# Two-layer steps of a conditional layer pair: the second gelu half ahead of x_hi on ScalarE, the second norm's statistics ahead of x_lo on VectorE

## What is computed

```python
out_nr  = gelu(x @ w1_nr + b1_nr) @ w2_nr + b2_nr          # out_tsr alike
out_sr  = gelu(gelu(x @ w1_sr + b1_sr) @ w2_sr + b2_sr) @ w3_sr + b3_sr
y = x + out[kind];  y = layernorm(y) * gamma + beta
h = gelu(y @ down_W.T + down_b)                            # 256 -> 64
h = h @ expert_W[e].T + expert_b[e] + domain_emb[e]
z = h @ up_W.T + up_b + y;  z = layernorm(z) * ln_gamma + ln_beta
```

## Time and profile before

| | |
|---|---|
| median of 3 runs | 278.79 us (278.51 to 279.04) |
| profiled execution | 277.94 us, its span 276.1 us |
| granted TensorE clock | 0.985 over the span, 1.00 in the two-layer steps from 120 to 240 us |
| PE busy | 252.9 us, 92% of the span |
| DVE busy | 203.0 us, 74% |
| ACT busy | 191.2 us, 69% |
| POOL busy | 174.7 us, 63% |
| chain that ended last | PE 58%, ACT 13%, issue 11%, DVE 8%, POOL 5% |

### The profile page before, as it was taken

The page is one execution under the profiler, slowest core; times in us unless marked ns, Lnnn a source line. Parts: engine busy times, 40 slices in busy tenths (PEclk is TensorE's granted clock), DMA queues, the critical chain, the costliest instruction groups (busy, mean ns, idle before and its releaser), DMA issues.

```text
span 276.1 us, 8026 instructions
## 1 busy us (share of the span) xinstructions
PE 252.9 (92%) x2114; PEld 219.2 (79%) x2115; DVE 203.0 (74%) x715; ACT 191.2 (69%) x450; POOL 174.7 (63%) x190
## 2 busy tenths in 40 slices
PE   7998999999999988999999999999999999999850
PEld 7798889989989977878887777788888888778630
DVE  6779453294495485878888877888888888878871
ACT  3587579668768765867777777777777777777730
POOL 3134565455876876867777677677776777677480
PEclk9999999999999999999999999999999999999995
DMA  6373011101212202232323222333232323222224
GB/s 181 101 251 70 6 36 42 23 22 40 61 39 58 67 28 57 67 85 80 91 76 95 76 76 79 83 85 82 80 85 77 94 76 95 76 77 71 54 66 92
DMA packets 41640, 20.71 MB, mean 75 GB/s; under 512 B 37431, under 2 KB 39181, under 8 KB 41614
## 3 DMA queue, kind: packets, MB, share of 16 engines
q1 hardware_dynamic: 37785, 12.23, 18.5%
q0 software_dynamic: 2592, 7.08, 7.3%
q10 hardware_dynamic: 1236, 1.06, 1.5%
HBM read 11.69 MB, written 8.65 MB: 74 GB/s over the span
## 4 chain that ended last, share of the span: by engine, by line
PE 58%; ACT 13%; issue 11%; DVE 8%; POOL 5%; DMA 2%; DVEq 1%; ACTq 1%; SPq 1%; POOLq 0%
PE ps_h L1082 18%; PE ps_z L1150 12%; PE ps_t L1172 9%; PE ps_z L1155 6%; ACT yt L931 5%; ACT x_hi L883 4%; ACT h_hi L897 3%; POOL h_lo L481 2%; PE ps_z L1117 2%; PE ps_u L1202 2%; PE ps_t L1253 2%; POOL rs L488 1%; PE ps_t L1256 1%; PE ps_t L1254 1%; DMA out<-o 1%
## 5 line engine op out<-in xcount | busy, mean ns | idle before, releaser
L481 POOL TENSOR_TENSOR h_lo<-h,h_hi 128x256 fp32r<-128x256 f32 (+1 forms) x75 | 70.6, 942 | 45.3 <-ACT h L897 42.1
L488 POOL TENSOR_TENSOR rs<-ve,minus_half 128x4 f32<-128x4 f32 (+1 forms) x38 | 41.0, 1079 | 32.2 <-DVE ve L699 32.0
L904 ACT ACTIVATE zn<-ps_z,nm,rs 128x256 f32<-128x256 f32 x66 | 33.7, 562 | 31.4 <-DVE nm L703 30.9
L687 DVE BATCH_NORM_STATS2 st<-ps_z 128x6 f32<-128x256 f32 x66 | 24.9, 418 | 31.5 <-PE ps_z L1155 31.5
L897 ACT ACTIVATE h_hi<-ps_h,per_feature_sb 128x256 fp32r<-128x256 f32 x84 | 38.9, 496 | 12.3 <-PE ps_h L1082 8.2
L931 ACT ACTIVATE yt<-ps_t,per_feature_sb 128x256 f32<-128x256 f32 x66 | 34.1, 574 | 17.5 <-PE ps_t L1172 17.4
L1150 PE MATMUL ps_z<-last_hi,h_hi 128*128 (+1 forms) x132 | 35.8, 305 | 6.7 <-ACT h_hi L897 6.7
L897 ACT ACTIVATE h<-ps_h,per_feature_sb 128x256 f32<-128x256 f32 x84 | 38.8, 498 | 0.0
L661 DVE TENSOR_TENSOR x_lo<-x,x_hi 128x512 fp32r<-128x512 f32 x33 | 23.5, 712 | 19.8 <-ACT x_hi L883 19.8
L1202 PE MATMUL ps_u<-tables,stack 65*64 x132 | 35.6, 392 | 0.3 <-ACT stack L915 0.3
L1202 PE MATMUL ps_u<-second_table,stack 65*64 65x256 f32 x132 | 35.5, 392 | 0.0
(11 more groups left out here) (150 smaller groups left out, 658.3 us busy)
## 6 DMA issues: line engine op xcount, KB each, us to landing
x<-in_x_feat SPq DMA_DIRECT2D x130, 64.0 KB
out<-o SPq DMA_DIRECT2D x20, 64.0 KB, 2.0
out<-o,out_rows_now POOLq DMA_INDIRECT x54
last_sb<-in_last_w SPq DMA_DIRECT2D x1, 768.0 KB, 5.0
w_sr_sb<-in_w_sr SPq DMA_DIRECT2D x1, 512.0 KB, 4.0
w_sr_sb<-in_w_sr ACTq DMA_DIRECT2D x1, 512.0 KB, 5.0
w_two_sb<-in_w_two SPq DMA_DIRECT2D x1, 512.0 KB, 5.6
per_unit_sb<-in_per_unit SPq DMA_DIRECT2D x1, 268.1 KB
```

The costliest lines, as they stand in the source:

```text
L481: pool.tensor_tensor(dst, full, high.bitcast(F32), ALU.subtract).then_inc(ready, 1)
L488: pool.tensor_tensor(RS[p][:, norms, :], VE[p][:, norms, :], half_of_two[:, norms, :], ALU.pow).then_inc(rstd, 1)
L904: ins = act.activation(ZN[:, t, :], ZP[p][:, t, :], ACT.Identity, bias=NM[p][:, t:t + 1], scale=RS[p][:, 0, t:t + 1])
```

## The change

On ScalarE, the two-layer branch makes the second gelu half before it makes x_hi of the slot after next. On VectorE, in all steps of the main loop and in LAST2, the second norm's statistics come before x_lo, and their aggregation stays behind it; in LAST2 the call to `last_variances` is written out accordingly. No instruction is added or taken away. The SR branch on ScalarE, and the programs of GpSimd, TensorE and SyncE, are as before.

```diff
                 for slot in on_slot(g, 0, where):
                     first_moments(slot, p)
                 variances(p, BOTH)
+                for slot in on_slot(g, 2, where):
+                    second_stats(slot, p)
                 for slot in on_slot(g, -2, where):
                     input_low(slot, p)
                 for slot in on_slot(g, 2, where):
+                    second_moments(slot, p, q)
                     if where == LAST2:
-                        last_variances(slot, p, q)
-                    else:
-                        second_stats(slot, p)
-                        second_moments(slot, p, q)
+                        dve.wait_ge(stat[1], 2 * TT * slot + 2 * TT)
+                        variances(q, SECOND)
@@
-                    next_input(g, i, p, where)
                     for k in kind:
                         second_of_two(k)
+                    next_input(g, i, p, where)
```

## The result

The changed kernel takes 272.1 us (median of 4 runs, 271.59 to 273.23), the kernel before, run beside it, 278.92 (278.51 to 279.66): a ratio of 0.9755, 95% interval 0.9731 to 0.978, or 6.8 us less. The profiled execution took 271.85, its span is 270.1 (before 276.1). The forecast was 274.1, the range 269.5 to 280.3.

A forecast was written before the change was run, and what follows sets the result against it. Two nearly level loops, TensorE's and GpSimd's with yt, were taken to bound the two-layer lap of 6.37. 277.94 - 5.0 (laps) + 0.3 (three-layer slots) = 273.2, plus 0.85 to the median: 274.1 us, range 269.5 to 280.3.

The forecast's parts named there:

- Two loops, nearly level, with x_hi in both: Two-layer steps: TensorE's loop and GpSimd's yt, h, h_lo, scatter, scatter, yt (6.37, the lap) run nearly level; both contain x_hi.
- The late release: End of the two-layer lap: yt starts 1.24 after its transposes, not 0.64, at a fixed 1.77 behind the second scatter.
- x_hi and the second half: ScalarE: high half moves to y + 0.91 (y: yt's start), x_hi to y + 1.65; lap 5.86 if nothing else binds, gain 0.51.
- what ve then holds up: VectorE to GpSimd: h_lo waits for rs, 5.80 after the previous lap's x_lo start; lap 6.06, gain at most 0.31.
- x_lo and h_lo meet: VectorE against GpSimd: where h_lo starts first, x_lo effectively starts 0.60 after it; such laps take 6.40.
- Mean of direct and meeting laps: Two-layer laps: mean of 5.86 and 6.40 is 6.13, 0.24 below 6.37, times 21 laps: -5.0 us.
- rival B: Late release goes away, yt follows transposes by 0.64: laps about 6.0, 271.3 us, fully 266.3; chance 0.19.
- Three-layer slots: VectorE, three-layer steps: x_lo put behind the statistics ends 0.05 to 0.1 late in four slots: +0.3 us.
- Tail: After the last input, which ends at the last but two step, the order stays: no change.
- The sum: Whole kernel: 277.94 - 5.0 + 0.3 = 273.2 profiled; with the median 0.85 above that execution, 274.1 us; chance 0.42.
- A: Rival: the two loops lock, x_lo meeting h_lo in every lap or alternating; no change, 278.9 us (278.3 to 279.7); chance 0.25.
- C: Rival, slower: first scatter stretched 0.18 by x_lo, yt 2.26 after the second scatter; lap 6.53, 282.5 us; chance 0.14.

## Why the prediction was right, and what it missed

*Two loops, nearly level, with x_hi in both.* Right that x_hi's 0.51 is not the price, as ScalarE's move alone shows. *The late release*, which the forecast took as given: it is real, and worth 0.55 a lap between the two kinds of chip, but it belongs to the chip. The forecast is right for a chip of that kind only.

*x_hi and the second half.* All starts within 0.02. TensorE's idle time before the last layer's high half is cut from 0.55 to 0.17; a wait of 0.25 before its low half has come in its place, for h_lo and so for rs, as "what ve then holds up" said.

*x_lo and h_lo meet.* The wait is the 0.60 of the earlier trace rows: x_lo's 1.24 less its 0.69 is 0.55, with 0.03 between the starts 0.58. A meeting lap from h_lo to h_lo was put at 6.40. Here it took 6.18 (157.65 to 163.83): what follows x_lo was shorter by 0.2 than taken.

*Mean of direct and meeting laps.* 6.13 forecast, 6.16 measured; -5.0 against -4.7. That it came so close is partly luck: the direct lap of 5.86, in which x_lo and h_lo miss each other, never occurred. In 15 of the 21 laps x_lo took 0.81 to 1.28, and in the other six x_lo ran first at its 0.68 and h_lo took 1.10 to 1.22. Laps do alternate, between 5.7 to 6.0 and 6.3 to 6.8 in the first half, wider later (5.29 and 7.00). In five of the short ones yt follows its transposes by 0.64 to 0.82, so that there the late release costs little or nothing, which was rival B's mechanism at part strength.

*Three-layer slots: +0.3.* Wrong in sign: -0.61 up to the first lap. "GpSimd's rs may gain there from not meeting x_lo; I count nothing" is the step that failed. In the transition, before and then after:

```profile
98.08 0.69 DVE L661 TENSOR_TENSOR x_lo<-x,x_hi 128x512 fp32r<-128x512 f32 x1
...
98.24 1.45 POOL L488 TENSOR_TENSOR rs<-ve,minus_half 128x4 f32<-128x4 f32 x1 [1.47 <-DVE ve L699]
```

```profile
97.94 1.04 POOL L488 TENSOR_TENSOR rs<-ve,minus_half 128x4 f32<-128x4 f32 x1 [1.36 <-DVE ve L699]
...
98.44 0.67 DVE L661 TENSOR_TENSOR x_lo<-x,x_hi 128x512 fp32r<-128x512 f32 x1
```

rs had started 0.16 behind x_lo and took 1.45; it now comes first and takes 1.04. That transition became 0.50 shorter (9.80 to 9.30 between two starts of yt), in the kernel with VectorE's move alone as well (9.29), and not with ScalarE's alone (9.79).

*Tail: nothing.* 0.66 less (0.23 + 0.43). I did not trace it. The 0.43 behind the last yt has another cause than the late release: on a chip that takes 266 this part is shorter too (14.05 to 13.51).

*The sum.* The forecast was 2.0 too high: about 0.9 from the three-layer slots and the transition, 0.7 from the tail, 0.6 because the 0.85 between the median and the profiled execution is 0.25 in the changed kernel, less 0.3 that the laps gained too little.

*Rivals.* A's meetings occur, its lock does not. C's first part is there (first scatters of 1.28), its second is not: yt comes 1.63 after the second scatter, not 2.26. The one step that C drew this from the earlier trace rows was misread: its first gelu was late not through TensorE's first layer but through the same hold. On a chip that takes 266 the matmuls of that step start within 0.01 us of the same times and the gelu starts 1.32 earlier, at 118.03 (here 119.35). What does make the change slower elsewhere was none of the rivals: where no release is late, the kernel before runs within 0.12 a lap of TensorE's shortest lap, and losses outweigh what is left to gain.

## What to carry to other kernels

Before an idle time is costed, compare the same pair of instructions in two steps: yt followed its transposes by 0.64 in one and 1.24 in another, and that difference, not the link on the chain, decided what the change was worth. An order tuned around such a wait can lose where the wait is absent, so try it on more than one chip. Two moves in one change can depend on each other: here one alone cost 3%, the other nothing, and both together gained 2.4%.

## What the hardware showed that was not expected

- **Chips differ in one wait.** Of five chips in the experiments one ran the kernel before in 279.1 us and four in 266.0 to 266.5, at the same granted clock (1.00 in the two-layer steps) and with three-layer steps equal to 0.2 us. Only on the first did TensorE's release reach ScalarE 0.60 late, beside the second indirect scatter: on the others the semaphores of that last first-layer matmul and of the transposes land 0.29 to 0.30 after the matmul's start in every lap. Why chips differ, and what besides the scatter it takes, stays open.
- **rs is stretched by x_lo, not the other way round.** With x_lo first, rs took 1.45; with rs first, x_lo kept its 0.67 to 0.69.
- **The scatters' own lengths vary.** The first took 1.04 in the earlier trace rows and 1.28 behind a late x_lo; the second 0.96, but 1.40 to 1.45 in nearly every second lap of the kernel before on a chip that takes 266 (158.75), at the same place in the program. Whether an instruction of VectorE does it, and which, was not sorted out.
